# Layer 3 of a four-element AdaLN kernel: the feed-forward residual rebuilt from normalised tokens and parameter rows, the attention gate folded into Wo, and new instruction orders

## The reference, cut to what matters

```
h = layernorm(x) * (1 + ca) + sa
x = x + ga * attention(h)
h = layernorm(x) * (1 + cb) + sb
x = x + gb * ffn(h)
```

```
o = o * sigmoid(h @ Wg.T + bg)
return o @ Wo.T + bo
```

```
last = h[:, -1, :]
logits = gelu(last @ Wp1 + bp1) @ Wp2 + bp2
sel = argmax(softmax(logits))
y = gelu(h @ W1[sel] + b1[sel]) @ W2[sel] + b2[sel]
return h + 0.3 * (y @ Wo + bo)
```

## Time and profile before

| | us |
|---|---|
| median of 3 runs | 1735.24 (1734.53 to 1736.05) |
| the profiled execution, its own time | 1735.68 |
| its span in the profile | 1733.9 |
| PE busy | 1698.8 |
| DVE busy | 1235.9 |
| POOL busy | 1218.6 |
| ACT busy | 1089.0 |

### The profile page before, as it was taken

The page is one execution under the profiler, slowest core; times in us unless marked ns, Lnnn a source line. Parts: engine busy times, 40 slices in busy tenths (PEclk is TensorE's granted clock), DMA queues, the critical chain, the costliest instruction groups (busy, mean ns, idle before and its releaser), DMA issues.

```text
span 1733.9 us, 31801 instructions
## 1 busy us (share of the span) xinstructions
PE 1698.8 (98%) x10006; PEld 1302.2 (75%) x10006; DVE 1235.9 (71%) x4490; ACT 1089.0 (63%) x2904; POOL 1218.6 (70%) x1771
## 2 busy tenths in 40 slices
PE   8999999999999999999999999999999899999998
PEld 5888888876667676676676777767788787788976
DVE  7954335688977988988899866445566766578773
ACT  6555226456677678777777886546546666665656
POOL 5655549898878987888799785135347876666667
PEclk9999999999999999999999999999999999999999
DMA  7100000010000000000000000000000001000002
GB/s 254 68 32 1 1 1 4 3 51 1 1 1 1 1 1 1 1 1 1 1 1 1 1 11 6 1 1 7 2 3 3 1 18 31 21 2 1 2 3 73
DMA packets 24027, 26.70 MB, mean 15 GB/s; under 512 B 3492, under 2 KB 20772, under 8 KB 23476
## 3 DMA queue, kind: packets, MB, share of 16 engines
q1 hardware_dynamic: 23860, 24.67, 4.6%
HBM read 22.52 MB, written 2.15 MB: 14 GB/s over the span
## 4 chain that ended last, share of the span: by engine, by line
PE 84%; DVE 5%; POOL 5%; ACT 4%; issue 2%; POOLq 0%; DVEq 0%; ACTq 0%
PE ps L87 77%; PE ps L90 7%; POOL arena L104 5%; ACT arena L98 3%; DVE arena L104 2%; DVE arena L110 1%; DVE arena L147 1%; DVE arena L130 0%; ACT arena L99 0%; ACT L98 0%; DVE arena L133 0%; DVE arena L107 0%; DVE arena L136 0%; DVE ps L147 0%; DVE ps L104 0%
## 5 line engine op out<-in xcount | busy, mean ns | idle before, releaser
L104 POOL TENSOR_TENSOR arena<-arena 128x512 f32<-128x512 f32 (+6 forms) x836 | 715.4, 869 | 277.7 <-DVE arena L110 96.5
L98 ACT ACTIVATE arena<-ps 128x128 f32<-128x128 f32 (+11 forms) x1204 | 338.8, 326 | 393.5 <-PE ps L87 285.2
L87 PE MATMUL ps<-arena 128*128 128x128 f32 (+4 forms) x2792 | 440.5, 291 | 9.1 <-DVE arena L104 3.8
L87 PEld LDWEIGHTS ps<-arena 128*128 128x128 f32 x2792 | 373.4, 192 | 96.0 <-issue 47.6
L104 DVE TENSOR_TENSOR arena<-ps,arena 128x128 f32<-128x128 f32 (+4 forms) x696 | 313.2, 469 | 175.7 <-PE ps L87 163.4
L98 ACT ACTIVATE arena<-arena 128x128 f32<-128x128 f32 (+1 forms) x836 | 321.2, 439 | 50.9 <-POOL arena L104 38.9
L87 PE MATMUL ps<-arena,moe 128*128 128x256 f32 (+1 forms) x960 | 288.2, 439 | 0.0
L87 PE MATMUL ps<-arena,cst 128*128 128x504 f32 (+2 forms) x768 | 283.8, 489 | 2.4 <-ACT arena L98 1.3
L98 ACT ACTIVATE arena<-ps,cols 128x512 f32<-128x512 f32 x324 | 216.8, 688 | 103.2 <-PE ps L87 96.3
L104 POOL TENSOR_TENSOR arena<-arena,cst 128x144 f32<-128x144 f32 (+7 forms) x536 | 186.2, 356 | 92.4 <-ACT arena L98 57.7
L110 DVE SCALAR_TENSOR_TENSOR arena<-ps,arena 128x128 f32<-128x128 f32 (+1 forms) x476 | 157.0, 365 | 119.6 <-PE ps L87 94.1
(11 more groups left out here) (120 smaller groups left out, 1761.9 us busy)
## 6 DMA issues: line engine op xcount, KB each, us to landing
rows<-in_rows SPq DMA_DIRECT2D x1, 2253.0 KB, 14.5
arena<-in_x SPq DMA_DIRECT2D x8, 256.0 KB, 5.2
wf<-in_wf SPq DMA_DIRECT2D x2, 1024.0 KB, 7.0
arena<-in_L_ffn_W SPq DMA_DIRECT2D x8, 256.0 KB, 3.0
out_dram<-arena SPq DMA_DIRECT2D x8, 256.0 KB, 2.7
wmod<-in_wmod SPq DMA_DIRECT2D x4, 384.0 KB, 8.1
arena<-kept SPq DMA_DIRECT2D x24, 64.0 KB, 3.0
arena<-kept SPq DMA_DIRECT2D x8, 192.0 KB, 3.2
```

The source lines that it names most:

```text
L87: return UNSENT if self.e is None else self.e.matmul(out, lhsT, rhs, start=start, stop=stop)
L98: return self.e.activation(out, in_, func, bias=bias, scale=scale)
L104: return UNSENT if self.e is None else self.e.tensor_tensor(out, a, c, op)
```

## The change

Four things are changed.

- **Feed-forward residual.** The transposition of `m.hT` back to tokens (8 PE transpositions and 2 ACT copies of 128x512 for each element) is gone. `m.xn` already holds the normalised tokens; POOL now forms `gb * h` from them as `xn * ((1 + cb) * gb)`, with the row product in `r.row(1)`, and `sb` goes into the bias row: `bor = (bor + sb) * gb`. Two more rows of each element have to be loaded for that: a new transfer `feat3_b` of 256 columns behind each `gain3_b`. The large POOL operations remain six for each element: two multiplications that can run before the expert is known, two additions of `m.bor` and two additions to `r.x`.
- **Gate in Wo.** POOL forms `m.wog = Wo * ga` and `r.row(2) = bo * ga` once for each element. Each group of four tiles gets the bias row added to `r.x` by one POOL operation of 128x512 (mark `e3start`); DVE then adds each tile's product straight from PSUM to `r.x`. Both POOL operations of each tile, and the wait for `e3out`, are gone.
- **Scratch.** `cc` shrinks from 44 to 34 columns and `m.wog` takes 128.
- **Order.** All four strings of `TURNS` are new. Fewer yields are needed: the strings have 3333 and 3295 digits for PE, 3861 and 3831 for DVE, 2145 and 2107 for ACT, 1180 and 1146 for POOL, before and after. By the change's own description only the turns of the first stage and of layers 2 and 3 were searched.

The diff, without the digits of `TURNS`:

```diff
@@ -358,7 +358,7 @@
         else:
             self.hT, self.DT, self.grow = self.a, r.take(512), r.take(512)
             self.S, self.R = r.take(128), r.take(128)
-            cc = r.take(44)
+            cc, self.wog = r.take(34), r.take(128)
             self.ss, self.rn, self.bt = cc[:, 0:4], cc[:, 4:8], cc[:, 12:16]
             self.ngcols = cc[:, 20:24]
             self.arow, self.above = G[:, 0:512], self.XT
@@ -389,113 +389,112 @@
 
 
 TURNS = {
...
 }
 
 
@@ -2264,7 +2263,8 @@
                     yield
                     pe.wait_ge(*at("e3oT", b, t))
                     ps = banks.take(pe, b, b, "e3p", t)
-                    pe.mm(ps[:, 0:128], m.oT, wsm("wo3")).then_inc(*pe.up(b, "e3p", b, t))
+                    pe.wait_ge(*at("e3wog", b))
+                    pe.mm(ps[:, 0:128], m.oT, m.wog).then_inc(*pe.up(b, "e3p", b, t))
                     yield
             leave(pe, b, "l3")
 
@@ -2414,9 +2414,7 @@
                     yield
                     ps = banks.get(b, "e3s", t)
                     dve.wait_ge(*at("e3s", b, t))
-                    if t:
-                        dve.wait_ge(*at("e3out", b, t - 1))
-                    elif g == 0 and i == 0:
+                    if t == 0:
                         dve.wait_ge(*at("e3gt", b, g))
                     dve.tt(m.sc, ps[:, 0:128], m.DT[:, c], ALU.mult).then_inc(
                         *dve.up(b, "e3sc", b, t, free=(b, "e3s", t)))
@@ -2429,8 +2427,9 @@
                     yield
                     ps = banks.get(b, "e3p", t)
                     dve.wait_ge(*at("e3p", b, t))
-                    dve.tt(m.sc, ps[:, 0:128], row("bo3"), ALU.add).then_inc(
-                        *dve.up(b, "e3wo", b, t, free=(b, "e3p", t)))
+                    dve.wait_ge(*at("e3start", b, g))
+                    dve.tt(r.x[:, t, :], r.x[:, t, :], ps[:, 0:128], ALU.add).then_inc(
+                        *dve.up(b, free=(b, "e3p", t)))
                     yield
             leave(dve, b, "l3")
 
@@ -2456,17 +2455,20 @@
                     c = col4(i)
                     if i == 0:
                         enter(pool, b, ("l3i", g))
+                        if g == 0:
+                            pool.wait_ge(*arrives(f"gate3_{b}"))
+                            pool.tt(m.wog, wsm("wo3"), r.row(2), ALU.mult).then_inc(*pool.up(b, "e3wog", b))
+                            pool.tt(r.row(2), row("bo3"), r.row(2), ALU.mult).then_inc(*pool.up(b))
+                            pool.wait_ge(*pool.last(b))
+                        yield
+                        xg = r.x[:, 4 * g:4 * g + 4, :]
+                        pool.tt(xg, xg, over(r.row(2)), ALU.add).then_inc(*pool.up(b, "e3start", b, g))
+                        yield
                     if t:
                         pool.wait_ge(*at("e3qT", b, g))
                         pool.wait_ge(*at("e3p", b, t - 1))
                         pool.tt(m.qg, m.qT[:, c], m.grow[:, c], ALU.mult).then_inc(*pool.up(b, "e3qg", b, t))
                         yield
-                    pool.wait_ge(*at("e3wo", b, t))
-                    pool.wait_ge(*arrives(f"gate3_{b}"))
-                    pool.tt(m.sc, m.sc, r.row(2), ALU.mult).then_inc(*pool.up(b))
-                    pool.wait_ge(*pool.last(b))
-                    pool.tt(r.x[:, t, :], r.x[:, t, :], m.sc, ALU.add).then_inc(*pool.up(b, "e3out", b, t))
-                    yield
             leave(pool, b, "l3")
 
 
@@ -2607,17 +2609,10 @@
             ps = banks.take(pe, b, b, "f3r")
             pe.mm(ps[:, 0:1], wsm("wp1"), m.hT[:, 1023:1024]).then_inc(*pe.up(b, "f3p", b))
             yield
-            for g in (1, 0):
-                if g == 0:
-                    pe.wait_ge(*at("f3av", b))
-                    pe.mm(ps[0:1, 8:16], m.av, wsm("wp2")).then_inc(*pe.up(b, "f3r", b))
-                    yield
-                    pe.wait_ge(*at("f3", "h", b, 0))
-                tps = banks.take(pe, b, b, "f3t", g)
-                for i in range(4):
-                    ins = pe.tr(tps[:, col4(i)], m.hT[:, 512 * g + 128 * i:512 * g + 128 * i + 128], ident)
-                ins.then_inc(*pe.up(b, "f3t", b, g))
-                yield
+            pe.wait_ge(*at("f3av", b))
+            pe.mm(ps[0:1, 8:16], m.av, wsm("wp2")).then_inc(*pe.up(b, "f3r", b))
+            yield
+            pe.wait_ge(*at("f3", "h", b, 0))
             for g in range(2):
                 for j in range(2):
                     yield
@@ -2657,17 +2652,9 @@
             act.wait_ge(*at("f3p", b))
             act.act(m.av, ps[:, 0:1], ACT.Gelu, bias=col("bp1")).then_inc(*act.up(b, "f3av", b))
             yield
-            for g in (1, 0):
-                ps = banks.get(b, "f3t", g)
-                act.wait_ge(*at("f3t", b, g))
-                act.act(m.xn[:, 512 * g:512 * g + 512], ps[:, :]).then_inc(
-                    *act.up(b, "f3xn", b, g, free=(b, "f3t", g)))
-                yield
-                if g:
-                    act.wait_ge(*at("f3sh", b))
-                    act.act(m.lg[0:1, :], m.lg[0:1, :], ACT.Exp, accum=m.sx[0:1, 0:1]).then_inc(
-                        *act.up(b, "f3ex", b))
-                    yield
+            act.wait_ge(*at("f3sh", b))
+            act.act(m.lg[0:1, :], m.lg[0:1, :], ACT.Exp, accum=m.sx[0:1, 0:1]).then_inc(*act.up(b, "f3ex", b))
+            yield
             for g in range(2):
                 for j in range(2):
                     yield
@@ -2729,23 +2716,35 @@
 
         def l3f_pool(b):
             m, r = Ffn3(room[b]), room[b]
+            enter(pool, b, "l3")
+            yield
+            scales_pool(b, "f3", "stats", b)
+            yield
+            pool.wait_ge(*arrives(f"gain3_{b}"))
+            pool.wait_ge(*arrives(f"feat3_{b}"))
+            pool.tt(r.row(1), r.row(1), r.row(5), ALU.mult).then_inc(*pool.up(b))
+            for g in (1, 0):
+                yield
+                tmp = four(m.xn[:, 512 * g:512 * g + 512])
+                pool.wait_ge(*at("f3", "n_act", b, g))
+                pool.wait_ge(*at("f3", "n_dve", b, g))
+                pool.wait_ge(*at("f3", "x", b, g))
+                pool.wait_ge(*pool.last(b))
+                pool.tt(tmp, tmp, over(r.row(1)), ALU.mult).then_inc(*pool.up(b))
+            yield
+            pool.wait_ge(*at("f3bor", b))
+            pool.tt(m.bor, m.bor, r.row(0), ALU.add).then_inc(*pool.up(b))
+            pool.wait_ge(*pool.last(b))
+            pool.tt(m.bor, m.bor, r.row(5), ALU.mult).then_inc(*pool.up(b))
             for g in range(2):
                 yield
-                if g == 0:
-                    enter(pool, b, "l3")
-                    scales_pool(b, "f3", "stats", b)
-                    yield
                 tmp = four(m.xn[:, 512 * g:512 * g + 512])
-                pool.wait_ge(*at("f3xn", b, g))
-                pool.wait_ge(*at("f3bor", b))
+                pool.wait_ge(*pool.last(b))
                 pool.tt(tmp, tmp, over(m.bor), ALU.add).then_inc(*pool.up(b))
-                pool.wait_ge(*pool.last(b))
-                pool.wait_ge(*arrives(f"gain3_{b}"))
-                pool.tt(tmp, tmp, over(r.row(5)), ALU.mult).then_inc(*pool.up(b))
                 pool.wait_ge(*pool.last(b))
                 xg = r.x[:, 4 * g:4 * g + 4, :]
                 pool.tt(xg, xg, tmp, ALU.add).then_inc(*pool.up(b, "f3start", b, g))
-                yield
+            yield
             leave(pool, b, "l3f")
 
 
@@ -2905,6 +2904,8 @@
         def queue_gain(b, l, after):
             sp.wait_ge(*at("left", after, b, "pool"))
             spread(f"gain{l}_{b}", b, l, 5, 6)
+            if l == 3:
+                load(f"feat{l}_{b}", room[b].mod[:, 0:256], kept[l, b, 384:640].partition_broadcast(128))
 
         def queue_first():
             xv = A["x"].rearrange("b (t p) d -> b p t d", p=128)
```

213 lines of the change are left out of this document (106 added, 107 removed).

## The result

The kernel after takes 1739.26 us (median of 13 runs, 1737.71 to 1742.11), the kernel before 1735.78 beside it: ratio 1.0022, 95% interval 1.0015 to 1.0030. The forecast was 1730.2 with a range up to 1736.5, so the prediction was wrong in its sign: 3.5 us slower instead of 5 faster, with an interval that excludes no change. Of the named cases the time is nearest to rival 3, but that rival's mechanism did not occur, as the rows show.

The account below looks back on a forecast made before the run. PE, busy 1698.8 of 1733.9 us, was taken as the bound. Terms -1.75 - 2.3 - 1.2 - 0.5 + 0.75 gave -5.0 us, from 1735.68 to 1730.7, median 1730.2; own range 1728 to 1732.5, 8-in-10 range 1724 to 1736.5.

Parts of the forecast that it names:

- rival 3: Slower, 1739 us: new orders outside the searched stages cost PE gaps between 350 and 1250; 13% chance.
- Orders: Outside layers 2 and 3, swapped neighbours in the new turns: taken as 0, between -2 and +4 us.
- Transpositions and copies before 1697: Layer 3's tail: four ACT copies counted in full, -2.3 us; 1.75 us of transpositions beside them not counted.
- gaps shrinking to 4: Expected sign: PE's gaps from 1668 to its full stretch should be about 4 us, against 5.6 before.
- Transpositions after 1697: In PE's full stretch at the end: 16 removed transpositions come off in full if POOL lets them, -1.75 us.
- Tile end: Last attention tile: DVE adds straight to r.x, so the last element's statistics start earlier, -1.2 us.
- Earlier gaps: PE's 2.6 us of gaps between 1500 and 1650: earlier products fill some, -0.5 us, between 0 and 2.6.
- New waits: Layer 3's attention: waits for POOL's gate-row operations e3wog and e3start taken as 0; 8.4 us if uncovered.
- Large operations beside the routers: First routers: POOL's 8 multiplications slow DVE's 1x8 scalar operations, +0.75 us, between 0 and 1.5.
- POOL's balance: POOL net 10.8 us lighter; 8 multiplications move earlier, taking 10 us from its last run and letting PE's 1.75 through.
- Transfers: Four more transfers of 128 KB, issued with the gain loads: nothing is late.
- Rival 2: No gain, 1734 us: the last element's chain sets the end, so sparing PE opens equal gaps; 22% chance.

Follow-up runs that it names:

- e1: Kernel after with the first stage's turns taken back to those of before: 1737.27 us, ratio 1.0002 to the kernel before.
- e2: Kernel after with all turns up to the middle of layer 1's expert part, about 1000 us in, taken back to before's: 1736.44 us, ratio 1.0001.
- e4: Kernel before with only the first stage's turns of the kernel after: 1739.38 us, ratio 1.0018.
- e7: Kernel after with 16 more warm-up products on PE ahead of the second modulation product at the start: 1737.31 us, ratio 1.0010 to the kernel before.
- e5: Kernel before in its own order with the feed-forward residual part of the change alone: 1740.68 us, ratio 1.0030.
- e9: e5 with POOL's two multiplications for each element moved right ahead of its addition to the output bias row: 1740.58 us, ratio 1.0033 to the kernel before.
- e8: e1 with 13 warm-up products in PE's waits in element 3's last attention tiles: 1734.48 us, ratio 0.9993 to the kernel before.
- e10: e8 with 5 warm-up products ahead of the second modulation product and 4 ahead of the first expert product: 1732.40 us, ratio 0.9988 to the kernel before.
- e14: Kernel after in its own order with 12 warm-up products at the start, 13 in element 3's last attention tiles, 4 before the first expert product: 1735.57 us, ratio 1.0003.
- e13: e6 without POOL's e3start additions and DVE's wait for them, gated bias row missing from the result: 1735.44 us, ratio 1.0002 to the kernel before.
- e6: Kernel before in its own order with the attention part of the change alone (gate in Wo, new tile end): 1738.95 us, ratio 1.0021.
- e11: e8 without POOL's e3start additions and DVE's wait for them, gated bias row missing from the result: 1733.48 us, ratio 0.9991 to the kernel before.
- e12: Kernel before with three warm-up products ahead of the last tile's update on PE: 1734.47 us, ratio 1.0001.

## Why the prediction was wrong

*Orders: taken as 0, with -2 to +4 for those outside layers 2 and 3.* The step that failed first. I argued from 350 to 1250, where it held (7.5 us of gaps in both, e1 equal to e2), and did not cost the first stage's new turns, which were part of the change. They put a statistics operation that waits for `x` ahead of the modulation columns in DVE's queue, and PE waits 4.3 us. e1, e4: 2 to 3.5 us. e7 gives some 2 of them to the clock; e4's executions, whose time does not follow their clock, do not bear that share out, so the split is open.

*Transpositions and copies before 1697: -2.3, and gaps shrinking to 4.* Failed: this is the step that a reader should take from this case. I read those gaps as time that spared work would shorten. In e5 the spared transpositions lay inside PE's waits; taking them out lengthened the waits, and stretches at half clock followed, in e9 too. With the clock held (e8, e10, e14) the way from element 0's last tile to element 3's is 23.4 to 23.5 us, against 23.9 before, and 23.5 in the profile after: 0.4 to 0.5 us gained where 3.5 were counted (copies and tile end). That the copies were hardly on the chain of the last tiles is how I read it; no run takes out the copies alone. The prediction also took this stretch for one in which all four elements are in the feed-forward part; in before's trace the last attention tiles of elements 1, 2 and 3 end at 1674.5, 1682.6 and 1690.8, and they are what fills it.

*Transpositions after 1697: -1.75.* The size is borne out in part: the stage from the last tile to the last product is 38.0 before, 36.3 after and 36.2 in e10 (-1.7, -1.8), but 36.6 in e8 and 37.2 in e14 (-1.4, -0.8), where PE waits 1.1 us for the first expert's load.

*Tile end: -1.2.* Right at its place, worth nothing at the end. In e13, which has this part alone, the last element's statistics are ready 2.6 us ahead of before's while everything around is 1.4 ahead: 1.2 us, as worked out. But PE's transpositions that use them come 1.4 ahead again: in e13 ACT works without a pause from 1691.4 to 1696.7 on other elements' activations, which stand ahead of this normalisation in its queue, and takes it up only then.

*Earlier gaps: -0.5, and POOL's new additions: 0.* Failed. Under "New waits" I asked who waits for these additions and what would be late if they were; I did not ask what stands behind them in POOL's queue (steps of the inverse, some 2 us) and on the shared port (one of DVE's scans, some 1): 3.2 us in the old order (e6, e13). In the searched order the stage is 2.0 longer, and the additions are 0.2 of it (e11). Whether the search chose a longer order to get past them, or this order is merely worse, is open: PE's idle time there is no larger than before's (147.91 us busy of the 150 from 1500, for 147.40 in the earlier trace rows), so the 2 us are spread over many slightly later starts inside what counts as busy. The kernel before in this order was not tried.

*Large operations beside the routers: +0.75.* Nothing came of it at the first routers. DVE's small scalar operation takes 262 ns in the stretch of 1680 to 1697, as in the earlier trace rows, and 491 in that of 1698 to 1716:

```profile
L107 DVE TENSOR_SCALAR arena<-arena 1x8 f32<-1x8 f32 x4 | 1.1, 262 | 0.0
...
L107 DVE TENSOR_SCALAR arena<-arena 1x8 f32<-1x8 f32 x4 | 2.0, 491 | 0.1
```

The exclusive lock that I cited and set aside shows at another place, the scan of e6.

*POOL's balance.* -10.9 us on the page for -10.8 forecast; but POOL's row ends 1.0 us ahead of the last addition instead of several, since it starts 4 us later (1702.5 for 1698.5). It did let most of PE's 1.75 us through. That the eight multiplications could stand earlier for nothing was an assumption: in the old order they held up ACT by way of the scales (e5, 1.8 us against e9). *Transfers: 0*, confirmed: no wait for a kept row shows.

*The rivals.* Rival 2 (1734, no gain, the chain of the last element sets the end) described the tail best: with the tail's clock held, e8, e10 and e14 lie at 1732.4 to 1735.6. The price that it names for after was missed all the same, since it knew nothing of the start, the attention and the clock. Rival 3 had the time but not the cause, so that it came near is luck. No case of mine had the granted clock as a term, though the row for it, 1.00 in every window of the earlier trace rows beside a PE with 5.6 us of gaps in 29, was in front of me.

Sum for the profiled execution, by stages: start +1.6, layer 2 +0.6 (with a half-clock stretch of 3.4 us), attention +2.0, its last tiles -0.4, tail -1.7: +2.0 within rounding. The medians are 3.5 apart since the profiled run is after's fastest: six of its 13 runs have a mean clock of 0.992 or 0.993 and take 1739.4 to 1742.1, the seven at 0.994 to 0.997 take 1737.7 to 1739.3.

## What to carry to other kernels

Where PE waits on chains between engines, work taken from PE inside those waits need not shorten anything, and here it was followed by stretches at half clock: look at what fills each gap before counting a removal, and try a few useless products there. A single profile can be the lucky one: look at the mean clock of all executions before taking its clock as the kernel's. When an operation is made large and moved to an engine with slack, ask not only who waits for it, but what is queued behind it and whom its port holds. A change that re-searches a fixed order is as large as the order: compare the first stage's waits first, where in this kernel PE waits for DVE and DVE for a transfer.

## What the runs showed of the hardware

- The granted clock fell to 1.2 GHz for 3.4 to 10.2 us in one piece, also between waits that are short. In e1 PE was busy for 5.3 of the 7 us up to 1680, with one wait of 1.35 us, and the clock fell at 1680.7. A single wait's length does not tell: before's tail has one of 1.06 us and kept 2.4 GHz in its profiled execution, while e5's first fall in the tail, at 1680.1, follows one of 0.73. The Trainium skill (TensorE: Matmul & The Clock Gate, part 1) has the clock halve for an idle PE; here it halved for a PE that was busy most of the time.
- Adding 13 to 29 bf16 products of about 0.25 us each to a kernel whose PE is busy for 98% of the span made it 1.6 to 3.3 us faster by the ratios (e7, e8, e14), and three brought nothing in a tail without half clock (e12).
- The length of layer 3's attention stage repeats to 0.1 us between builds and runs (157.6, 159.6, 160.8), which tells more apart than medians of executions that spread by 4 us. The first stage does not: in the old order and without warm-up products there its mark lies between 355.9 and 357.4, with no order in how long the clock was halved.
